# A decoder layer on one core: a new order of steps on all engines at the end of the kernel

## The reference

```python
x = _layernorm(x + _L0_attn_ref(x, ...))              # a selective state-space scan (Mamba)
x = _layernorm(x + _L0_xattn_ref(x, ctx_512, ...))    # cross attention, 16 heads, low-rank keys and values
x = _layernorm(x + _L0_ffn_ref(x, w_up, w_down))      # feed-forward net with quantised activations
```

## Time and profile before

| | us |
|---|---|
| three runs | 511.55, 515.33, 512.59 |
| their median | 512.59 |
| the profiled execution | 515.37 |
| its span in the profile | 513.6 |
| last instruction ends | 511.43 |

### The profile page before, as it was taken

One profiled execution on the slowest core, in us unless ns is written; L12 is line 12 of the kernel. 1 busy time (PEld: TensorE's weight loads), 2 busy tenths in 40 slices (PEclk: granted clock), 3 DMA queues, 4 the chain that ended last, 5 costly groups with the idle time before them and its releaser, 6 DMA issues.

```text
span 513.6 us, 11539 instructions
## 1 busy us (share of the span) xinstructions
PE 412.5 (80%) x4148; PEld 336.5 (66%) x4148; DVE 391.2 (76%) x744; ACT 295.3 (58%) x699; POOL 216.1 (42%) x157
## 2 busy tenths in 40 slices
PE   3988962765785838779989999999999999995742
PEld 1435631645574738658878888888888888884531
DVE  0876878996999987998485477878787887874564
ACT  2535997795999978996034353544535353543420
POOL 1400005994979794978323332422324132420100
PEclk9989995696989989999999999999999999998865
DMA  8960364114301241011300000000000000000000
GB/s 282 359 279 13 131 197 133 31 38 97 114 31 38 63 158 40 23 41 43 128 1 4 11 3 1 23 3 0 20 0 20 0 20 0 20 0 1 20 1 21
DMA packets 18659, 30.94 MB, mean 60 GB/s; under 512 B 2113, under 2 KB 11713, under 8 KB 17921
## 3 DMA queue, kind: packets, MB, share of 16 engines
q1 hardware_dynamic: 18624, 30.49, 18.0%
HBM read 24.16 MB, written 6.32 MB: 59 GB/s over the span
## 4 chain that ended last, share of the span: by engine, by line
PE 56%; DVE 15%; ACT 12%; issue 10%; DMA 5%; POOL 1%; SPq 1%; DVEq 0%; POOLq 0%; ACTq 0%
PE ps L437 46%; PE ps L559 5%; ACT hc L923 4%; PE ps L670 3%; ACT ps L915 3%; DVE reg_b L1343 2%; DMA ud_t<-ud_dram 2%; DVE ps L1336 2%; DVE reg_b L1277 1%; DMA xw<-x_fm 1%; DVE reg_b L1230 1%; ACT reg_b L895 1%; DMA reg_a<-rope_q 1%; POOL reg_b L1136 1%; PE ps L711 1%
## 5 line engine op out<-in xcount | busy, mean ns | idle before, releaser
L1136 POOL TENSOR_TENSOR reg_b<-reg_c,reg_a 128x1024 f32<-128x1024 f32 x56 | 130.4, 2369 | 61.4 <-DVE reg_c L1282 61.2
L1159 POOL TENSOR_TENSOR reg_b<-reg_b 128x768 f32<-128x768 f32 x32 | 57.9, 1810 | 118.3 <-DVE reg_b L1415 118.3
L437 PE MATMUL ps<-x1T,Mw 128*128 (+1 forms) x768 | 93.1, 278 | 1.0 <-DVE reg_b L1415 1.0
L437 PEld LDWEIGHTS ps<-x1T,Mw 128*128 128x128 f32 x768 | 88.3, 192 | 3.7 <-issue 1.7
L559 PE MATMUL ps<-ident,hc 128*128 128x128 f32 x456 | 70.7, 301 | 16.8 <-ACT hc L923 15.5
L923 ACT ACTIVATE hc<-reg_b,bc 128x512 f32<-128x512 f32 x96 | 69.0, 719 | 17.2 <-PE ps L559 13.9
L559 PEld LDWEIGHTS ps<-ident,hc 128*128 128x128 f32 x456 | 57.2, 155 | 27.6 <-ACT hc L923 24.7
L1343 DVE SCALAR_TENSOR_TENSOR reg_b<-reg_c,bc,ps 128x512 f32<-128x512 f32 x96 | 70.1, 735 | 0.0
L915 ACT ACTIVATE ps<-reg_b 128x512 f32<-128x512 f32 x112 | 65.7, 593 | 7.5 <-POOL reg_b L1136 7.5
L1336 DVE TENSOR_TENSOR ps<-ps,reg_b 128x512 f32<-128x512 f32 x80 | 54.7, 689 | 9.1 <-ACT ps L915 9.1
L1141 POOL TENSOR_TENSOR small<-small 128x1 f32<-128x1 f32 x24 | 13.3, 555 | 95.4 <-DVE small L1361 95.4
(11 more groups left out here) (150 smaller groups left out, 701.6 us busy)
## 6 DMA issues: line engine op xcount, KB each, us to landing
reg_a<-a_dram SPq DMA_DIRECT2D x4, 1024.0 KB, 7.6
Mw<-w_o SPq DMA_DIRECT2D x1, 2048.0 KB, 15.7
ud_dram<-reg_b SPq DMA_DIRECT2D x4, 512.0 KB, 4.3
zs_dram<-x1T SPq DMA_DIRECT2D x4, 512.0 KB, 3.7
ud_t<-ud_dram SPq DMA_DIRECT2D x8, 256.0 KB, 3.0
zs_t<-zs_dram SPq DMA_DIRECT2D x8, 256.0 KB, 2.7
xw<-x_fm SPq DMA_DIRECT2D x2, 512.0 KB, 7.1
mring<-w_q SPq DMA_DIRECT2D x4, 256.0 KB, 4.0
```

The costliest lines, as they stand in the source:

```text
L437: return pe.matmul(o, l, r, start=start, stop=stop)
L1136: pool.tensor_tensor(dA[:, g % RING], delta_r[:, bass.ds(t, 1), :].to_broadcast([P, SA, DI]), Abc[:, g * SA:(g + 1) * SA, :], ALU.mult).th ...
L1159: pool.tensor_tensor(rq[:, g % 2].rearrange("p a c n -> p (a c n)"), pc[:, g % 2].rearrange("p a c n -> p (a c n)"), psn[:, g % 2].rearran ...
```

## The change

Every piece stands in the end of the kernel, but for one swap in ACT's slots and one in SP's loop.

- PE: the last scores, of step 31, go to the first halves of banks 0 and 1, which `project` has left (`scores_at`); they wait for `ropem` (the last `rope` has read these banks) and no longer for `soft(30)`. The last tile's merge goes to the second half of bank 2. `scores(30)` stands ahead of `to_latent(31)`, `turn_prob(30)` ahead of `ffn(6, 5)`, `context(31)` and the last `merge_group` ahead of `ffn(6, 7)`.
- ACT: in slots with g = 3 `soft(k - 2)` stands ahead of `take_ctx(k - 3)`; at the end `take_prob(30)` stands ahead of `ffn(6, 5)`, `take_ctx(31)` ahead of `ffn(6, 7)`.
- DVE: after the loop `normalize(29)` and `norm2_stats(6)` stand ahead of `row_max(30)`; near the end `ffn(7, 9)` stands ahead of `ffn(6, 12)`, and `ffn(7, 10)` ahead of `norm3_rows(6)`. A wait for `x3_s` is added to `ffn(7, 12)`; the instruction that it waits for stands earlier on the same engine.
- SP: each x1 tile is asked for before the store of the tile two back, not after it (two loads ahead of the first store).

```diff
-        last_work = (ps[:, 0, :], ps[:, 1, 0:DM], rope_words[0][:, 0:256].rearrange("p (k n) -> p k n", k=KM),
+        last_work = (ps[:, 0, :], ps[:, 2, DM:2 * DM], rope_words[0][:, 0:256].rearrange("p (k n) -> p k n", k=KM),
...
+        scores_last = ps[:, 0:2, 0:256].rearrange("p e (i n) -> p e i n", i=2)
+
+        def scores_at(k):
+
+            return scores_last if isinstance(k, int) and k == G * T - 1 else scores_of
...
             stage_x1(0)
-            with sp.Fori(1, T) as t:
+            stage_x1(1)
+            with sp.Fori(2, T) as t:
                 stage_x1(t)
-                store(t - 1)
+                store(t - 2)
+            store(T - 2)
             store(T - 1)
...
             def scores(k, t, g):
                 pe.wait_ge(qev, k + 1)
-                need(pe, pexp, k)
+                if isinstance(k, int) and k == G * T - 1:
+                    pe.wait_ge(ropem, G * T)
+                else:
+                    need(pe, pexp, k)
...
-                        last = mm(scores_of[half, e, i, :], qk[rows, g % 2, i, half], kvT_step[rows, :])
+                        last = mm(scores_at(k)[half, e, i, :], qk[rows, g % 2, i, half], kvT_step[rows, :])
...
             last = G * T - 1
+            scores(last - 1, T - 1, G - 2)
             to_latent(last, G - 1)
-            scores(last - 1, T - 1, G - 2)
             ffn(T - 3, 11)
             turn_prob(last - 2, T - 1, G - 3)
             scores(last, T - 1, G - 1)
             ffn(T - 3, 12)
             context(last - 2, T - 1, G - 3)
-            pe.wait_ge(ropem, G * T)
             merge_group(T - 1, 0)
+            turn_prob(last - 1, T - 1, G - 2)
             ffn(T - 2, 5)
-            turn_prob(last - 1, T - 1, G - 2)
-            ffn(T - 2, 6)
             context(last - 1, T - 1, G - 2)
             merge_group(T - 1, 1)
+            ffn(T - 2, 6)
             turn_prob(last, T - 1, G - 1)
             merge_group(T - 1, 2)
+            context(last, T - 1, G - 1)
+            merge_group(T - 1, 3)
             ffn(T - 2, 7)
-            context(last, T - 1, G - 1)
             ffn(T - 2, 8)
-            merge_group(T - 1, 3)
...
-                if begun(k - 3):
-                    take_ctx(k - 3, t if g == 3 else t - 1, (g + 1) % G)
+                if begun(k - 3) and g < 3:
+                    take_ctx(k - 3, t - 1, (g + 1) % G)
                 if begun(k - 2):
                     soft(k - 2, (g + 2) % G)
+                if begun(k - 3) and g == 3:
+                    take_ctx(k - 3, t, 0)
...
             soft(last, G - 1)
+            take_prob(last - 1, G - 2)
             ffn(T - 2, 5)
-            take_prob(last - 1, G - 2)
             take_ctx(last - 1, T - 1, G - 2)
             take_prob(last, G - 1)
+            take_ctx(last, T - 1, G - 1)
             ffn(T - 2, 7)
-            take_ctx(last, T - 1, G - 1)
...
+                    if isinstance(t, int) and t == T - 1:
+                        dve.wait_ge(x3_s, T - 1)
...
             last = G * T - 1
+            normalize(last - 2, G - 3)
+            norm2_stats(T - 2)
             row_max(last - 1, G - 2)
-            norm2_stats(T - 2)
-            normalize(last - 2, G - 3)
...
             ffn(T - 2, 10)
+            ffn(T - 1, 9)
             ffn(T - 2, 12, T)
             norm3_stats(T - 2)
-            ffn(T - 1, 9)
+            ffn(T - 1, 10)
             norm3_rows(T - 2)
-            ffn(T - 1, 10)
```

More of the change, by code:

```diff
@@ L1018, in soft @@
                 for h in range(HG):
-                    last = act.activation(prob[:, g % 2, h, :], scores_of[:, h % 2, h // 2, :], ACT.Exp,
+                    last = act.activation(prob[:, g % 2, h, :], scores_at(k)[:, h % 2, h // 2, :], ACT.Exp,
                                           bias=negm[:, g % 2, h:h + 1], accum_out=sums[:, g % 2, h:h + 1])
@@ L1419, in row_max @@
                 need(dve, pexp, k - 1)
-                dve.tensor_reduce(negm[:, g % 2].rearrange("p (i e) -> p e i", e=2), scores_of, AX.X,
+                dve.tensor_reduce(negm[:, g % 2].rearrange("p (i e) -> p e i", e=2), scores_at(k), AX.X,
                                   ALU.max, negate=True).then_inc(mx, 1)
```

## The result

The changed kernel took 500.96 us (median of 500.88, 501.58, 501.04 and 500.04), the kernel before beside it 512.26 (median of four). The ratio is 0.9744, with an interval of 0.9708 to 0.9781; that is 13.1 us of 512.3. The profiled execution took 500.88 us, its last instruction ends at 496.95, and 511.43 was it before: 14.48 us less.

A forecast was written before the change was run, and what follows sets the result against it. PE bounds the loop; after it, two chains in which engines wait for each other. 7.1 + 3.2 + 0.2 = 10.5 us less gives 502.1 from the median; 503 taken, own range 499.5 to 506, eight-in-ten range 499.5 to 507.5.

The forecast's parts named there:

- the loop: All tiles before the end: PE has no wait to remove except 0.19 us in tile 2; 0.2 us gained.
- the second chain: Tile 7's feed-forward net after its opening add: DVE's step 9 moves into a wait, 3.2 us less.
- The step from sum to time: Whole kernel: 502.1 us from the median, or 504.6 if the median run had no slow-clock stretch; middle taken, 503.
- the slow stretch: PE at 1.2 GHz after the gaps around one set of transposes, near 473 to 475 us; costs 2.5 us.
- First chain: Attention of steps 30 and 31, from tile 6's last merge to tile 7's add: 7.1 us less.
- The cover of 0.5 us: ffn(6, 7) and (6, 8) behind the last merge: squares done near 480.4, wanted about 480.9, so no cost.
- SP's load at nothing: SP's earlier x1 load: worth nothing, as it would land near 476.5 anyway, ahead of the add at 477.9.
- From 503.36 to the end: Last stretch, after step 12 of tile 7's Hadamard to the last DVE instruction: 8.07 us, unchanged.
- The clock falls again: Rival: remaining gaps slow PE's clock after 470.4 us, adding 4 or 5 us; 507.5 us, chance 0.12.
- full clock in the second chain: Lower bound of the forecast's own range: PE keeps full clock in tile 7's net, 2.5 us down.
- The swap starves the loop: Rival: late row maxima hold soft on ACT and delay take_ctx in every tile; 518 us, slower chance 0.03.
- The first chain does not shorten: Rival: an unseen wait sets PE's pace after the loop, only the swap near the end pays; 509.4 us, chance 0.07.

The follow-up runs named there:

- e1: The kernel before with only the swap in ACT's slots (soft ahead of take_ctx at g = 3): 512.22 us, ratio 0.9960.
- e2: The changed kernel with the swap in ACT's slots taken back: 504.25 us, ratio 0.9815.
- e7: The kernel before run again without an edit, for a second profile: 514.20 us, ratio 0.9996.
- e10: The kernel before with unread matmuls added in PE's gaps around turn_prob(29): 511.99 us, ratio 0.9968.
- e3: The changed kernel with the last scores in banks 4 and 5 again, waiting for soft(30): 503.84 us, ratio 0.9819.
- e9: The changed kernel with DVE's three steps after the loop in the old order, row_max(30) first: 503.05 us, ratio 0.9782.
- e6: The changed kernel with ffn(6, 7) and (6, 8) ahead of the last merge, as before: 501.79 us, ratio 0.9743.
- e4: The changed kernel with SP's loop as before, x1 load asked for after the store: 501.66 us, ratio 0.9747.
- e5: The changed kernel with DVE's order near the end as before, ffn(6, 12) ahead of ffn(7, 9): 504.94 us, ratio 0.9824.
- e8: The changed kernel with unread matmuls added where PE idles near the end: 498.53 us, ratio 0.9722.
- e11: The changed kernel run again without an edit: 500.63 us, ratio 0.9747.

## Why the prediction was right and wrong

**The sum as a whole.** 10.5 us were forecast on the path and 13.1 measured; the direction and the two main terms held. By the ratio the time to set against my 503 us is 0.9744 x 512.59 = 499.5, at the lower end of my range. Of these 3.5 us the loop makes 1.3, the second chain 0.8, the first 0.3 and the end 0.2; the last 0.9 come from the step from sum to time.

**The step that failed** is the loop: "in the loop PE has no wait to remove. I take 0.2 us." It was 1.5 us. I read idle times, and there are none; the waits lay inside the modelled length of the matmuls. My own remark that `row maxima were there 3.7 us before the merge's end` (3.63 by the rows: 464.87 - 461.24) was the hint: `soft` could have run then and ran only behind the merge, and the same wait of 5.40 us stands in the middle of the loop (before the copy at 349.45 us). The rows to look at were the starts of `normalize`, the weight load and the transposes in the first slot. e1 and e2 put 1.4 to 1.5 us on this swap. In place of "no wait" the traces show, in each of tiles 4 to 7, transposes that start 0.12 us late and a first slot that is 0.18 us longer.

**The step from sum to time failed too.** I had 502.1 by the sum from the median and took 503, the middle between it and 504.6, in case the median run lacked the slow stretch. e7 shows that stretch again, and e1, whose end is in the old order too, shows it a third time (granted clock 0.50 from 468 to 472 us). Three of three profiled executions have it, so there was no ground for the 0.9 us that I added. What varied is the moment of the fall and how much the stretch cost (19.81, 20.15 and 21.37 us for the first chain), not whether it was there. The Trainium skill ("TensorE: Matmul & The Clock Gate", section "What's actually happening") says that the moment at which the clock changes varies from run to run. The two traces of the kernel before agree with that: it fell behind the transposes of step 29 in one (0.66 us) and ahead of them in e7 (1.11 us). That is no ground to expect the stretch to be absent. Its price was not 2.5 us in that execution either, but 1.8 (e10). From the last scores to the end of the merge of group 0 the slow steps took 2.16 us more (473.23 to 478.09, against 471.51 to 474.21), and part of that covered a wait for ACT that e10 shows behind it.

**First chain, 7.1 forecast, 7.38 measured.** By its parts it held: `scores(30)` at once behind the merge, the last scores 2.5 us after it (464.50 - 461.96; forecast 2.4), the clock full. Those parts are tested: the score banks are worth 1.9 us (e3), the ACT swap 1.9 (e2), DVE's new head 1.5 (e9), the place of `ffn(6, 7)` and `(6, 8)` 1.25 (e6). They overlap and should not be added up. The cover of 0.5 us that I gave the last of these was enough: in the trace after, tile 6's squares end at 477.14 and DVE begins step 9 at 477.66, without a wait. Not tested alone are `scores(30)` ahead of `to_latent(31)` and `turn_prob(30)` ahead of `ffn(6, 5)`.

**SP's load at nothing** was right (e4).

**Second chain, 3.2 forecast, 4.0 measured.** The mechanism was right (e5 returns the 3.26 us wait), its size too small. I let the Hadamard of tile 7 start after DVE's step 12. PE does not wait for that step: it began at 487.09 right behind its own matmuls for step 12, while DVE's row is at 487.34. So step 12 to the row max is 1.71 us, where I had 2.11: 0.4. The rest is shorter distances ahead of it, 5.22 against 5.40 to `quantize_in` and 7.39 against 7.60 to step 12, of the size by which the clock's place in them can shift them (the first of them is 5.49 us in e6 and 4.72 in e8, where the clock is full). "From 503.36 to the end, 8.07 us, nothing changes" was 0.17 off. It lies in the last transposes of step 11: from their start to ACT's copy it is 0.64 us before (clock 0.50), 0.56 in e11 and 0.48 after (clock 1.00 from 490 to 492 us), and the stretches are 8.07, 7.99 and 7.90. I had not reckoned with another clock there.

**The rivals.** *The clock falls again*: it did not in the first chain, and e3 shows it full even behind a wait of 2.18 us. It fell in the second chain, as before. My other bound, full clock in the second chain, was "2.5 us down"; e8 measures 1.8. *The swap starves the loop*: the opposite. *The first chain does not shorten*: no. Of my marks for the changed trace, "the add of tile 7 on DVE at 477.5 to 478" was missed at 474.73: 1.4 us of it is the scan, 1.5 the loop, 0.3 the chain. The marks for the scores and for the end (496.95, where I had 501) were missed by the same terms.

## What to carry to other kernels

Where an engine looks busy without a gap, compare the distance between starts of the same two steps, slot by slot: a wait can lie inside a modelled matmul, and 0.18 us per tile add up. When a change moves a step on one engine in a loop, write down when its consumer's input arrives, when the consumer's weight load starts, and when its first matmul does. The distance from input to load alone does not tell: it is 0.22 us in the first slot before, and only 0.05 in the second, where nothing is lost, as the load there still starts 0.09 us ahead of its matmul (358.53 and 358.62). In the slot that loses time the load has no head start. And cut traces into stretches between fixed instructions: here, in two executions of one kernel, each repeated to 0.1 us but for the scan and the stretches with the slow clock, while whole times vary by 1.5 us (the four runs of the kernel after) to 5.2 (the runs of the kernel before beside e3: 512.58 to 517.74).

## What was unexpected in the hardware

- A wait of 2.18 us of PE left the clock full (e3), while 2.60 and 2.13 us around one set of transposes brought 1.2 GHz in both executions of the kernel before and in e1.
- Unread matmuls in the gaps kept the clock at 2.4 GHz, and what stood on the path won 1.8 us in e8 and 1.8 to 3.0 in e10. They cost the chain nothing that shows.
- The same slow stretch cost different amounts in two executions of one kernel: 20.15 and 21.37 us for the same chain, and 18.34 and 17.93 for the one behind it.
